# Batch 0's ctx and half of W land in memory of later operands; layernorm coefficients, q1T copies and column sums change engines

## What is computed

```python
x1 = fake_quant(layernorm(x))        # round(x/s1 + z1) clipped to 0..255, back to float
x2 = fake_quant(ctx)                 # (2, 1024, 1024)
x  = x + tanh(g_xattn) * matmul(x1, x2)

y  = layernorm(x)
base = y @ W_base.T + b_base         # W_base is 1024 x 1024
gate = softmax(y @ W_gate.T)         # 8 experts
thr  = sigmoid(y @ W_thr + b_thr) * 0.125
w = relu(gate - thr) / its row sum (1 where that is 0)
moe  = einsum(y @ A_w, w, B_w) * 2   # rank 16 for each expert
x  = x + tanh(g_ffn) * (base + moe)
```

## Time and profile before

| | |
|---|---|
| median of three runs | 196.7 us (196.3 to 197.4) |
| the profiled execution | 196.47 us |
| its span | 194.4 us |
| PE busy | 177.1 us, 91% |
| DVE, ACT, POOL busy | 112.9, 85.4, 89.4 us |
| mean granted PE clock | 0.991 |
| moved by DMA | 22.77 MB |

### The profile page before, as it was taken

One profiled execution on the slowest core, in us unless ns is written; L12 is line 12 of the kernel. 1 busy time (PEld: TensorE's weight loads), 2 busy tenths in 40 slices (PEclk: granted clock), 3 DMA queues, 4 the chain that ended last, 5 costly groups with the idle time before them and its releaser, 6 DMA issues.

```text
span 194.4 us, 3050 instructions
## 1 busy us (share of the span) xinstructions
PE 177.1 (91%) x1135; PEld 155.3 (80%) x1135; DVE 112.9 (58%) x246; ACT 85.4 (44%) x126; POOL 89.4 (46%) x128
## 2 busy tenths in 40 slices
PE   0484999989999899999999899999999999999992
PEld 0483644658899899999974369999999999999991
DVE  1574699989788967748894482673612512503303
ACT  2249991666794576495581105220610420500300
POOL 3384494690202587764999689065400400400400
PEclk9997899999999999999999999999999999999999
DMA  6997689995775017120010000000202002002003
GB/s 224 313 400 248 148 265 350 416 400 174 233 225 187 0 20 252 55 108 0 3 70 40 0 3 0 0 0 0 111 0 108 0 3 108 0 0 108 5 0 108
DMA packets 9470, 22.77 MB, mean 117 GB/s; under 512 B 743, under 2 KB 2151, under 8 KB 9456
## 3 DMA queue, kind: packets, MB, share of 16 engines
q1 hardware_dynamic: 9442, 22.58, 33.7%
q10 hardware_dynamic: 14, 0.00, 0.0%
HBM read 18.39 MB, written 4.19 MB: 116 GB/s over the span
## 4 chain that ended last, share of the span: by engine, by line
PE 58%; DVE 16%; POOL 9%; ACT 7%; issue 5%; DMA 2%; ACTq 1%; DVEq 0%; POOLq 0%
PE bank L902 15%; PE bank L904 15%; PE bank L903 15%; POOL colacc L354 7%; PE bank L795 4%; DVE q L589 3%; PE bank L890 3%; DVE st L567 3%; DVE WTl L617 2%; DMA rt<-in_L_ffn_b_thr_dram 2%; ACT q2u L421 2%; PE bank L923 2%; DVE xs L603 2%; PE bank L925 2%; PE bank L924 2%
## 5 line engine op out<-in xcount | busy, mean ns | idle before, releaser
L902 PE MATMUL bank<-WTh,lnTh 128*128 128x388 f32 (+1 forms) x192 | 67.4, 351 | 0.0
L903 PE MATMUL bank<-WTl,lnTh 128*128 128x388 f32 (+1 forms) x192 | 65.2, 339 | 0.0
L904 PE MATMUL bank<-WTh,lnTl 128*128 128x388 f32 (+1 forms) x192 | 65.1, 339 | 0.0
L371 POOL TENSOR_TENSOR xs<-xs,tb 128x1024 f32<-128x1024 f32 x8 | 19.3, 2412 | 45.0 <-ACT xs L428 45.0
L902 PEld LDWEIGHTS bank<-WTh,lnTh 128*128 128x128 f32 x192 | 36.1, 188 | 0.7 <-DVE lnTl L617 0.2
L903 PEld LDWEIGHTS bank<-WTl,lnTh 128*128 128x128 f32 x192 | 36.2, 188 | 0.0
L904 PEld LDWEIGHTS bank<-WTh,lnTl 128*128 128x128 f32 x192 | 36.1, 188 | 0.0
L795 PE MATMUL bank<-q,q1T 128*128 128x512 bf16 x128 | 29.3, 379 | 0.3 <-ACT q1T L436 0.2
L354 POOL TENSOR_TENSOR colacc<-colacc,q 128x512 f16<-128x512 f16 x18 | 23.6, 1311 | 5.6 <-DVE q L589 4.1
L653 DVE SCALAR_TENSOR_TENSOR xs<-bank,con,xs 128x250 f32<-128x250 f32 (+2 forms) x24 | 12.7, 569 | 23.1 <-PE bank L925 17.5
L795 PEld LDWEIGHTS bank<-q,q1T 128*128 128x128 bf16 x128 | 12.1, 98 | 14.7 <-ACT q1T L436 0.9
(11 more groups left out here) (92 smaller groups left out, 219.7 us busy)
## 6 DMA issues: line engine op xcount, KB each, us to landing
ring<-in_ctx_dram SPq DMA_DIRECT2D x16, 512.0 KB, 6.6
xs<-in_x_dram SPq DMA_DIRECT2D x8, 512.0 KB, 6.9
ring<-in_L_ffn_W_base_dram SPq DMA_DIRECT2D x8, 512.0 KB, 5.7
out_dram<-xs SPq DMA_DIRECT2D x7, 512.0 KB, 2.6
tb<-in_L_ffn_b_base_dram SPq DMA_DIRECT2D x1, 512.0 KB, 6.2
ring<-in_L_ffn_A_w_dram SPq DMA_DIRECT2D x1, 512.0 KB, 6.3
ring<-in_L_ffn_B_w_dram SPq DMA_DIRECT2D x1, 512.0 KB, 3.9
out_dram<-xs SPq DMA_DIRECT2D x1, 194.0 KB, 2.5
```

The source lines that it names most:

```text
L371: nc.gpsimd.tensor_tensor(xs[:, t, :], xs[:, t, :], tb[:, :], ALU.add).then_inc(xb_ready, 1)
L902: mm(o, hi, WTh[:, k, a:b], start=(k == 0), stop=False, skip_group_check=True)
L903: mm(o, hi, WTl[:, k, a:b], start=False, stop=False, skip_group_check=True)
L904: ins = mm(o, lo, WTh[:, k, a:b], start=False, stop=(k == KT - 1), skip_group_check=True)
```

## The change

1. **Landing.** WTl, BTh, BTl, lnTh and lnTl, which are written only later, move to the end of SBUF, and a view over the same memory (`landing`) takes batch 0's ctx chunks and W blocks 4 to 7, each with a semaphore of its own. The ring holds A, the gates, W 0 to 3, then B and batch 1's ctx. SP issues x tiles 0 to 3, ctx 0 to 7, A, gates, all of W, x tiles 4 and 5, B, the bias, x tiles 6 and 7, ctx of batch 1. None of the loads up to x tile 5 waits for anything.
2. **Coefficients.** DVE does the epsilon add and the product with the mean behind each aggregation (`ln_inputs`, three linked or following instructions); POOL keeps the power and one or two short instructions. `-1/s1` (NR1) is made on DVE ahead of tile 0's aggregation.
3. **Order on ACT and DVE.** ACT takes ctx chunk 0 ahead of q1 tile 1, chunk 1 ahead of the copy of q1T tile 1, and the scaling of the bias moves behind the tenth of the late splits. DVE rounds q1 tile 0 ahead of the statistics of x tile 2, and copies q1T tiles 2 and 3 itself.
4. **Product.** PE begins the product with q1 tiles 0 and 1 alone, for chunks 0 and 1, between the transposes; two of the four `keep_busy(6)` go.
5. **Column sums.** POOL adds all eight chunks of batch 0, and the eight matmuls for h = 1 become one. `column_sums(0, 0)` stands behind chunk 6 as before; `column_sums(0, 1)` stands behind chunk 7 and ahead of everything else of the second half.

The diff, cut to its core:

```diff
-    chunks = [("ctx", c) for c in range(CPB)] + [("A", 0), ("gates", 0)]
-    chunks += [("W", o) for o in range(O // P)] + [("B", 0)]
+    OWN_W = 4
+    chunks = [("A", 0), ("gates", 0)] + [("W", o) for o in range(OWN_W)] + [("B", 0)]
     chunks += [("ctx", c) for c in range(CPB, B * CPB)]
...
+        own_home = {("ctx", c): landing[:, c * WC + GP:c * WC + GP + 2 * H] for c in range(CPB)}
+        own_home["W", OWN_W] = landing[:, after_WTl:after_WTl + D]
...
+            for c in range(CPB):
+                load_own(("ctx", c))
+            for n in range(NS):
                 load(n)
-            for n in range(n_first, len(chunks)):
+            for o in range(OWN_W, O // P):
+                load_own(("W", o))
+            load_x(MT)
+            load_x(MT + 1)
+            load(NS)
...
-                pool.wait_ge(moments[i], t + 1)
-                mean, var = mv[:, i, t, 0:1], mv[:, i, t, 1:2]
+                pool.wait_ge(moments[i], 2 * (t + 1))
...
-            for c in range(CPH):
+            for c in range(CPB):
                 sum_k(c)
             add_columns(0)
...
             affine_q1(0)
-            affine_q1(1)
-            affine_q1(2)
             act.wait_ge(s_recip, 2)
             affine_ctx(0)
+            affine_q1(1)
             copy_q1T(0)
+            affine_ctx(1)
+            copy_q1T(1)
+            affine_q1(2)
             affine_q1(3)
...
+            ln_inputs(0, 0)
             nc.vector.reciprocal(R2, S2).then_inc(s_recip, 1)
+            ln_moments(0, 1, (1,))
+            round_q1(0)
+            ln_moments(0, 2)
+            round_q1(1)
+            round_ctx(0)
...
+                    if k2 == 2 and b == 0:
+                        column_sums(0, 0)
+                if b == 0:
+                    column_sums(0, 1)
                 for m in range(1, MT):
...
-                if (b, h) == (0, 1):
-                    pe.wait_ge(q2_ready, (b * NH + h + 1) * CPH)
-                    for k in range(KT):
-                        ins = mm(pb[:, :], ones_b[:, :], q2[:, k, h * H:(h + 1) * H], start=(k == 0), stop=(k == KT - 1))
-                else:
-                    pe.wait_ge(col_added, (b + h + 1) * (KT - 1))
-                    ins = mm(pb[:, :], ones_h[:, :], colacc[:, h, :], start=True, stop=True)
-                ins.then_inc(flipped, 1)
+                pe.wait_ge(col_added, (b * NH + h + 1) * (KT - 1))
+                mm(pb[:, :], ones_h[:, :], colacc[:, h, :], start=True, stop=True).then_inc(flipped, 1)
...
+            product_chunk(0, (0, 1))
+            flip_q1(2)
+            product_chunk(1, (0, 1))
+            flip_q1(3)
+            product_chunk(0, (2, 3))
+            row_sums(0)
+            product_chunk(1, (2, 3))
+            for k2 in range(2, CPH):
+                product_chunk(k2, range(MT))
```

More of the change, by code:

```diff
@@ L159, in gated_block, with home @@
         gt = sb("gt", [P, 2, 64])
+        with nc.sbuf_tensor("landing", [P, KT * WC + 2 * O + 4 * D], F32) as landing:
+            pass
+        WTl = sb("WTl", [P, KT, WC], F32R)
+        BTh = sb("BTh", [P, O], F32R)
+        BTl = sb("BTl", [P, O], F32R)
+        lnTh = sb("lnTh", [P, 2, D], F32R)
+        lnTl = sb("lnTl", [P, 2, D], F32R)
+        after_WTl = KT * WC
+        own_home = {("ctx", c): landing[:, c * WC + GP:c * WC + GP + 2 * H] for c in range(CPB)}
+        own_home["W", OWN_W] = landing[:, after_WTl:after_WTl + D]
+        own_home["W", OWN_W + 1] = landing[:, after_WTl + O:after_WTl + O + D]
+        own_home["W", OWN_W + 2] = landing[:, after_WTl + 2 * O + D:after_WTl + 2 * O + 2 * D]
+        own_home["W", OWN_W + 3] = landing[:, after_WTl + 2 * O + 3 * D:after_WTl + 2 * O + 4 * D]
+        def home(key):
+            return own_home[key] if key in own_home else ring[:, slot_of[key], :]
         bank = [es.enter_context(nc.psum_tensor(f"bank{i}", [P, H], F32)) for i in range(8)]
@@ L165, in gated_block @@
         ones_row = gt[0:1, :, :].rearrange("p a b -> p (a b)")
-        (R1, R2, TGX, TGF, SS, CA, D1, D1C, RROW, BROW, NBT, Z1D, D2) = [con[:, i:i + 1] for i in range(13)]
+        (R1, R2, TGX, TGF, SS, CA, D1, D1C, RROW, BROW, NBT, Z1D, D2,
+         NR1) = [con[:, i:i + 1] for i in range(14)]
         s_scales = sem("s_scales")
@@ L417, in affine_ctx @@
                 arrived(act, ("ctx", c))
-                s = ring[:, slot_of["ctx", c], :]
+                s = home(("ctx", c))
                 if c >= NU:
@@ L484, in _ @@
             nc.scalar.activation(TGF, GF, ACT.Tanh).then_inc(s_tanh, 1)
-            affine_ctx(1)
-            copy_q1T(2)
-            copy_q1T(3)
-            for c in range(2, CPB):
+            for c in range(3, CPB):
                 affine_ctx(c)
@@ L654, in finish @@
                                                    op0=ALU.mult, op1=ALU.add).then_inc(out_part, 1)
-            ln_moments(0, 0)
+            for h in range(NH):
+                half_stats(0, 0, h)
+            half_stats(0, 1, 0)
             dve.wait_ge(scales_spread, 1)
@@ L796, in product_step, with product_chunk, first_half @@
                           q2[:, k, h * H:(h + 1) * H], start=(k == 0), stop=(k == KT - 1))
-            def first_half(b, after_chunk):
+            def product_chunk(k2, tiles):
+                pe.wait_ge(q2_ready, k2 + 1)
+                for m in tiles:
+                    pe.wait_ge(q1T_copied, m + 1)
+                    for k in (2 * k2, 2 * k2 + 1):
+                        ins = product_step(0, m, k)
+                    if k == KT - 1:
+                        ins.then_inc(prod_ready, 1)
+            def first_half(after_chunk):
+                b = 1
                 for k2 in range(CPH):
```

98 lines of the change are left out of this document (53 added, 45 removed).

## The result

The changed kernel takes **205.04 us** (median of four runs, 204.52 to 206.53), the kernel before 196.54 beside it (196.3 to 197.4): a ratio of 1.045, 95% interval 1.042 to 1.048. It is slower by 8.5 us. Forecast were 201.8 us and a range up to 203.6. The sign and the mechanism came out; the size is over the range.

The account below looks back on a forecast made before the run. The prediction took a full TensorE queue from the large product on as the bound, so only the head could change: 4.7 us for late adds plus 0.6 for the clock, 5.3 on 196.5, gave 201.8 us, range 198.0 to 203.6.

Parts of the forecast that it names:

- which term decides: Head: GpSimd's fourteen adds ahead of the one second-sum matmul end at 39.2, making the large product start 4.7 us late.
- Rival A: Head: the sums come in time, adds ending at 34.6, flips starting at 35.0; 196.4 to 196.9 us; chance 0.12.
- The walk: Head: step-by-step forecast of VectorE's and GpSimd's queues, adds from 17.9 to 39.2, chunk 7 rounded at 32.9.
- the turns: Head: GpSimd's adds and VectorE's roundings alternate under a lock; a met rounding takes 1.56 us and costs the adds 0.4.
- The landing: Head: transfers landing in memory of their own, without waits for ring slots, were to gain 0.
- the clock: TensorE's granted clock falls around its longer stand before the flips: 0.6 us taken, bounds 0 and 1.1.
- if the clock is down for 3 us of them: Clock step: 3 us at the lower clock lose 1.5 us of TensorE's work, 0.4 of it under VectorE's splits.
- rival C: Head: constants blocked three times, copies 1.4, clock 1.1; fourteenth add at 41, 203.6 us or more; chance 0.14.
- the start of the adds: Head: GpSimd's first chunk add, after the coefficients of all four x tiles, at 17.4 to 17.9; 17.9 taken.
- the price behind the head: After the large product starts: the moved bias scaling and the second batch together were to cost 0.
- the second batch's coefficients: Second batch: same queues with coefficients a little shorter, cost 0.
- The bias: Scaling moved behind ten late splits pushes the first gate and two splits by 1.14 us; cost 0, up to 0.3.

Follow-up runs that it names:

- e1: The changed kernel with the second column sum (h = 1) back on TensorE in eight matmuls, GpSimd adding only chunks 0 to 3: 197.01 us, ratio 1.003.
- e2: The kernel before with only the column-sum part of the change: GpSimd adds eight chunks, one matmul makes the second sum: 204.82 us, ratio 1.041.
- e7: The kernel before with only the landing part of the change, memory views and order of loads: 196.12 us, ratio 0.9995.
- e11: e3 plus the 44 unread matmuls of e10 between the q1 transposes: 203.05 us, ratio 1.036.
- e3: The changed kernel with 42 small unread matmuls ahead of the second column sum, keeping TensorE busy through half of the wait: 202.5 us, ratio 1.029.
- e13: e10 with the new coefficient split kept in the head alone and the code of before for later tiles: 196.28 us, ratio 0.999.
- e10: e1 with 44 more unread matmuls keeping TensorE busy between the q1 transposes: 196.73 us, ratio 1.001.
- e12: e10 with the bias loaded and scaled early again, ahead of the first splits: 196.7 us, ratio 1.000.
- e8: The changed kernel with product tiles m = 2 and 3 of the second half ahead of the second column sum: 203.23 us, ratio 1.034.
- e9: e1 with the bias, VectorE's constants and ScalarE's tanh early again, plus the unread matmuls of e10: 197.21 us, ratio 1.005.

## Why the prediction was right and where it failed

**Right: which term decides, and its place.** Fourteen adds ahead of one matmul, released by GpSimd, TensorE standing for some 5 us before it (forecast 5.3, measured 4.82), flips, scaling and column add late by it. e1 and e2 take it out and put it in alone. Rival A would have had the adds end at 34.6; they ended at 40.38. The walk through the queues was close at its ends: the last adds 8.02 for six as in the second batch before, and 40.38 - 18.96 = 21.4 us from first to fourteenth add where the walk had 39.2 - 17.9 = 21.3. Two roundings that met adds took 1.58 and 1.64 where the turns gave 1.56, and 0.69 where none was met. The Trainium skill ("SBUF — State Buffer", section "SBUF: two separate sides") states an exclusive lock for the port pair of the two engines; these rows agree with it in the new order too. The landing was worth 0 as forecast (e7). The early start of the product wasn't tried alone; in the changed kernel the clock's fall that comes with it is covered (e11).

**Luck: chunk 7, rounded at 32.8 where 32.9 was forecast.**

```profile
27.41 5.36 DVE L628 TENSOR_SCALAR q<-q2u 128x1024 bf16<-128x1024 uint8 x4
```

Chunk 3 was done at 27.3 instead of 26.4, and the last four roundings took 5.4 us instead of 6.5. The walk let every one of them meet an add; GpSimd was dry from 25.97 to 27.38, so the first of them took 0.68 us and only the other three 1.64 each. The two errors cancel.

**Failed: the clock, 0.6 taken, 1.1 as the upper bound, 2.5 measured.** The step was "if the clock is down for 3 us of them". The trace of before has one fall of about that length (from 17.2 to 20.6), and the prediction took the length over to a longer stand. It was down for ten, from 39 to 49.5, over the end of the stand and then the whole train of flips, so that 8.09 us of queue became 11.30; e3, which keeps TensorE at work for half of the stand and changes nothing else, gives back 2.5 us by medians (3.9 in the traces). Even rival C, which was to gather every mishap, had only "all of 1.1". With 2.5 in place of 0.6 the same sum gives 203.7.

**Failed in size: the start of the adds, 18.96 instead of 17.9.** Chunk 0 landed later than the 10.67 that the prediction took from the trace of before, and ScalarE took it at 11.46, the latest of all traces in which it takes this chunk second (the others: 10.27 to 11.34):

```profile
11.46 1.24 ACT L444 ACTIVATE q2u<-landing,prm,con 128x1024 uint8<-128x1024 f32 x1 [1.70 <-DMA landing<-in_ctx_dram]
```

GpSimd's power of x tile 3 thus started at 17.06 instead of 16.5. From there the three operations took 1.9 us (0.92, 0.63 and 0.34, the first two under VectorE's roundings) where 1.4 were allowed. Together 1.1 us. In e3, without the late fall of the clock, the last add ends at 40.02, 0.8 behind the forecast, and the large product starts 51.07 - 45.33 = 5.7 us late, against 4.7 forecast.

**Failed in its reason: the price behind the head, 0 taken, 0.6 measured.** The prediction gave the second batch's coefficients as "a little shorter" because it looked at GpSimd, who has time there, and not at VectorE, on whom the work was put and who is waited for at B. The bias, of which it did allow up to 0.3, was not the main one. The tails, and e13's wait against e10's and e12's, show it. That its scaling "delays nobody" was not so either: it sat at 63.69, not near 58, and VectorE waited 1.38 us for the gate's exponential behind it, 0.39 before; but e12, with the scaling early, gained nothing measurable.

Put together by medians: 5.4 for the adds (forecast 4.7), 0.6 behind the head (0), 2.5 for the clock (0.6) are the 8.5 us. The first of them is what is left, 6.0 of e3 less the 0.6 of the tails; no run measures it alone.

## What to carry to other kernels

Before giving an engine a sum that another one makes in 2 us, walk that engine's queue to its last instruction and ask who stands behind the result: here 1.89 us of matmuls were saved for 4.8 us of standing and half-speed work behind it. Price a new stand of TensorE with the clock down over all of the work that follows it, not over the length of the last fall seen. Short operations that need the result of the one before them cost its time too (0.26 us for a tile here), so count them on the engine that gets them, everywhere that the helper is called.

## What the hardware showed that was not expected

- **The granted clock came back after some three us in one place and after ten in another.** Before, it fell at about 17.2 and was back at 1.00 by 21, with TensorE busy for nearly all of that time. In the changed kernel it was 0.50 from 40 to 49 with TensorE busy for 3.47, 4.00 and 1.00 us of windows of 4, 4 and 1, and in e8 its mean was still 0.59 from 48 to 52, the last of the twelve microseconds after a stand of 3.2, with TensorE busy for 3.81, 2.13 and 3.55 us of the three windows. A single stand of 2.04 us left it at 1.00 (e3), and two of 1.78 and 2.36 with 2.5 us of work between them ended in 0.51 (e11). What decides that isn't settled here.
- **Where the clock can fall in the head, runs scatter by it.** e1's runs lie at 196.4 to 197.1 with a mean clock of 0.991 or more and at 199.1 to 199.7 with 0.981 or less. 44 matmuls that nothing reads made the spread 0.8 us in e10, but it was 3.4 in e9, 2.3 in e12 and 1.9 in e13 with the same ones.
- **A one-column power on GpSimd took 0.92 us and a product 0.63 while VectorE was rounding**; without a rival the power had taken 0.57 and such a product 0.19.
